# A selective scan's decay kept in PSUM: the exponential written over its input, three banks deep

## The reference, cut to what matters

```python
xn = layernorm over channels; each image gives 4 sequences (16 channels each) of 3136 tokens
xi, z = split(in_proj(xn));  u = silu(causal_conv4(xi) + conv_b)
dt, B, C = split(x_proj(u)); delta = softplus(dt_proj(dt) + dt_proj_b)
# per token, inner channel d (32) and state n (16):
dA = exp(delta * A);  h = h * dA + delta * u * B;  y = sum_n(h * C)
out = xn + out_proj((y + u * D) * silu(z))
```

## Time and profile before

| what | us |
|---|---|
| median of 3 runs | 11573.08 |
| lowest and highest | 11567.66, 11573.26 |
| span of the profiled execution, first to last instruction | 11567.8 |
| VectorE busy in it | 9091.6 |
| TensorE busy in it | 9063.4 |
| GpSimd busy in it | 7746.9 |
| ScalarE busy in it | 5494.1 |

### The profile page before, as it was taken

One profiled execution on the slowest core, in us unless ns is written; L12 is line 12 of the kernel. 1 busy time (PEld: TensorE's weight loads), 2 busy tenths in 40 slices (PEclk: granted clock), 3 DMA queues, 4 the chain that ended last, 5 costly groups with the idle time before them and its releaser, 6 DMA issues. The chain is left out here.

```text
span 11567.8 us, 144078 instructions
## 1 busy us (share of the span) xinstructions
PE 9063.4 (78%) x34187; PEld 4489.7 (39%) x34187; DVE 9091.6 (79%) x10036; ACT 5494.1 (47%) x9098; POOL 7746.9 (67%) x4490
## 2 busy tenths in 40 slices
PE   9967777777777777777777777777777799999997
PEld 9922222222222222222222222222222259996997
DVE  7769999999999999999999999999999912221222
ACT  0345555555555555555555555555555502320332
POOL 0059999998989999999989898999989800000000
PEclk9978888888888888888888888888888899999998
DMA  9611010101111111101010111111110110012002
GB/s 175 172 41 30 26 32 24 33 25 30 26 30 26 30 28 27 30 25 33 23 34 24 31 28 28 29 28 29 27 31 24 43 46 0 0 26 59 0 0 44
DMA packets 644710, 403.63 MB, mean 35 GB/s; under 512 B 399312, under 2 KB 631120, under 8 KB 643664
## 3 DMA queue, kind: packets, MB, share of 16 engines
q1 hardware_dynamic: 407888, 318.19, 11.0%
q10 hardware_dynamic: 236032, 77.08, 2.9%
HBM read 136.43 MB, written 103.80 MB: 21 GB/s over the span
## 5 line engine op out<-in xcount | busy, mean ns | idle before, releaser
L627 POOL TENSOR_TENSOR prod<-hs,bsp 128x448 f32<-128x448 f32 x3584 | 6395.7, 1817 | 333.9 <-PE ps L637 224.9
L615 DVE TENSOR_TENSOR_SCAN hs<-da,hs,dbu 128x448 f32<-128x448 f32 x3072 | 4423.0, 1440 | 0.0
L595 ACT ACTIVATE da<-ps,nega 128x448 f32<-128x448 f32 x3586 | 2201.2, 632 | 1741.2 <-PE ps L578 1607.3
L587 PE MATMUL ps<-stack,seld 96*128 96x448 bf16 x3586 | 1488.3, 415 | 1855.6 <-DVE dbu L605 1835.4
L605 DVE TENSOR_TENSOR dbu<-ps,bsp 128x448 f32<-128x448 f32 x3585 | 2148.5, 599 | 413.1 <-PE ps L587 398.1
L637 PE MATMUL ps<-prod,wc 128*32 128x448 f32 x7200 | 1763.8, 658 | 330.2 <-POOL prod L627 325.2
L587 PEld LDWEIGHTS ps<-stack,seld 96*128 96x128 bf16 x3586 | 357.1, 100 | 3753.0 <-DVE dbu L605 3284.4
L877 PE MATMUL ps<-pv,ws 128*128 128x224 f32 x8800 | 1692.3, 354 | 9.4 <-ACT pv L1030 7.1
L877 PEld LDWEIGHTS ps<-pv,ws 128*128 128x128 f32 x8800 | 1656.6, 188 | 45.7 <-issue 7.8
L578 PE MATMUL ps<-stack,seld 96*128 96x448 bf16 x3587 | 1482.0, 413 | 68.1 <-ACT da L595 67.8
L1211 DVE SCALAR_TENSOR_TENSOR pv<-ps,R 128x224 f32<-128x224 f32 x880 | 422.2, 480 | 1279.3 <-PE ps L877 1279.3
(11 more groups left out here) (120 smaller groups left out, 9271.4 us busy)
## 6 DMA issues: line engine op xcount, KB each, us to landing
stack<-parts SPq DMA_DIRECT2D x2700, 56.0 KB, 2.0
lnx<-in_x SPq DMA_DIRECT2D x118, 224.0 KB, 2.5
lny<-y_nchw SPq DMA_DIRECT2D x118, 224.0 KB, 2.7
x_column_pairs<-otile SPq DMA_DIRECT2D x225, 116.0 KB, 1.7
xpad<-x_column_pairs SPq DMA_DIRECT2D x32, 812.0 KB, 4.4
xpad<-in_x SPq DMA_DIRECT2D x64, 392.0 KB, 6.7
y_pairs<-yout ACTq DMA_DIRECT2D x32, 784.0 KB, 6.8
yin<-y_pairs SPq DMA_DIRECT2D x32, 784.0 KB, 4.4
```

Source lines behind the costliest of these rows:

```text
L587: pe.matmul(ps[:, DU_BANK + j % 2, 0:T], seld[0:96, b, :], stack[:, st.t % 2, 1, grp, :], start=True, stop=True).then_inc(S["du_spread"], 1)
L595: a.activation(da[:, j % 8, :], ps[:, D_BANK + j % 2, 0:T], ACT.Exp, scale=nega[:, j:j + 1])\
L615: v.tensor_tensor_scan(hs[:, j, :], da[:, j % 8, :], dbu[:, j % 8, :], 0.0 if first else hs[:, j, T - 1:T], ALU.mult, ALU.add)\
L627: g.tensor_tensor(prod[:, j % 8, :], hs[:, j, :], bsp[:, st.t % 2, 1, :], ALU.mult)\
```

## The change

The exponential is written in place, over its input in PSUM, and the scan reads it there. Three banks (0 to 2) take the part of two banks and of the eight SBUF buffers `da`, which go. As unit i of a round of 224 uses bank i % 3 and 224 is no multiple of 3, `d_bank_back` finds how many units back a bank was used last: three, and at the start of a round two (units 0, 1) or five (unit 2). `spread_delta` now waits for the scan of that unit and no longer for an exponential; `decay` waits for its matmul alone. To free a bank, `project_out` writes to bank 7, which the state sums (`Y_BANK`) now use too, and the first matmul of the sums also waits for the copies out of that bank. `project` moves from TensorE's step 8 to step 5, `sum0` from 7 to 8, and `evacuate` from ScalarE's step 12 to step 6.

```diff
-PE_AT = {0: ["bc0", "last3"], 3: ["bc1"], 5: ["lnc"], 7: ["sum0"], 8: ["project", "lnv"], 10: ["tap0", "tap2"],
+PE_AT = {0: ["bc0", "last3"], 3: ["bc1"], 5: ["project", "lnc"], 8: ["sum0", "lnv"], 10: ["tap0", "tap2"],
          12: ["tap1"], 13: ["tap3", "sum1", "z", "dt"], 14: ["sum2"]}
-ACT_AT = {1: ["bc0"], 2: ["relu"], 4: ["bc1"], 5: ["cast0"], 7: ["cast1"], 8: ["lnc"], 11: ["lnv"],
-          12: ["shift", "evacuate"], 14: ["silu", "u", "z", "exp"], 15: ["dt"]}
+ACT_AT = {1: ["bc0"], 2: ["relu"], 4: ["bc1"], 5: ["cast0"], 6: ["evacuate"], 7: ["cast1"], 8: ["lnc"], 11: ["lnv"],
+          12: ["shift"], 14: ["silu", "u", "z", "exp"], 15: ["dt"]}
...
-            da = sb(m, "da", [P, 8, T])
...
-        D_BANK, DU_BANK, TMP_BANK, Y_BANK, O_BANK = 0, 2, 4, 6, 7
+        D_BANK, DU_BANK, TMP_BANK, Y_BANK, O_BANK = 0, 3, 5, 7, 7
+        ROUND = ST * UN
+
+        def d_bank(st, j):
+
+            return D_BANK + (st.t * UN + j) % 3
+
+        def d_bank_back(st, j):
+
+            i = st.t * UN + j
+            back = [m for m in range(i - 5, i) if (m % ROUND) % 3 == i % 3]
+            return i - back[-1]
...
-            pe.wait_ge(S["exp_done"], st.tile * UN + j + 1)
-            pe.matmul(ps[:, D_BANK + j % 2, 0:T], seld[0:96, b, :], stack[:, st.t % 2, 0, grp, :],
+            pe.wait_ge(S["scan_done"], st.tile * UN + (j + 9 - d_bank_back(st, j)))
+            pe.matmul(ps[:, d_bank(st, j), 0:T], seld[0:96, b, :], stack[:, st.t % 2, 0, grp, :],
...
-            a.wait_ge(S["scan_done"], n + 1)
-            a.activation(da[:, j % 8, :], ps[:, D_BANK + j % 2, 0:T], ACT.Exp, scale=nega[:, j:j + 1])\
+            d = ps[:, d_bank(st, j), 0:T]
+            a.activation(d, d, ACT.Exp, scale=nega[:, j:j + 1])\
...
-            v.tensor_tensor_scan(hs[:, j, :], da[:, j % 8, :], dbu[:, j % 8, :],
+            v.tensor_tensor_scan(hs[:, j, :], ps[:, d_bank(st, j), 0:T], dbu[:, j % 8, :],
...
                 pe.wait_ge(S["y_gated"], tile + 2)
+                pe.wait_ge(S["out_evac"], tile * 2 + 3)
```

## The result

| | us |
|---|---|
| kernel before, median of 4 | 11573.17 |
| changed kernel, median of 4 | 11782.98 |
| ratio, with its 95% interval | 1.0184 (1.0169 to 1.0198) |
| span of the profiled execution | 11783.4 |

The forecast was 11280 us, faster. The kernel became 210 us slower; the time lies inside the range, the direction is wrong.

The account below looks back on a forecast made before the run. VectorE was taken as the bound, its scans taking turns with GpSimd's multiplies. Own work 29.9, full-clock waits 4.1 and low-clock waits 2.7 gave 36.7 us a tile against 37.96, hence 11280 us; range 10850 to 11920.

Parts of the forecast that it names:

- own work: VectorE's operations in one tile without its waits for TensorE, forecast at 29.9 us a tile.
- Part 1: Scan's first input moves to PSUM: scan and drive together fall from 1.88 to 1.57 us, 16 save 5.0 us a tile.
- turn: VectorE operations with two SBUF inputs and GpSimd's own exclude each other; scan and multiply about 0.95 us each.
- Part 2: TensorE's new wait for a scan delays drive: 4.1 us a tile at full clock, 2.7 us extra at lower clock.
- step 10: Two taps on TensorE, covered by VectorE's scale in half the tiles: 0.4 us of full-clock wait a tile.
- steps 13, 0, 5, 8, 10: Full-clock waits behind TensorE's tasks: 2.8, 0.6, 0, 0.1 and 0.4 us a tile, in that order.
- low-clock and round shares: Extra TensorE waits: 2.7 us a tile from 1.2 GHz, 0.2 from bank reuse where a 14-tile round ends.
- step 8: TensorE's sum0 and lnv, 2.4 us, partly covered by rest at 1.35: 0.1 us full-clock wait, 1.2 extra at low clock.
- the gap between project and sum0: Three steps now part these TensorE tasks; before, they adjoined and brought the clock up. Low clock adds 2.7 us a tile.
- Rival A: TensorE's queue becomes the bound, at steps 5 to 13: 40.0 us a tile, +460 us, about 12030 us; chance 0.26.
- B: TensorE's clock stays up, the low-clock extra goes: 34.0 us a tile, -890 us, about 10680 us; chance 0.14.
- C: The scan keeps taking turns with GpSimd despite PSUM: 41.3 us a tile, +740 us, 12310 us; chance 0.05.

Follow-up runs that it names:

- the first experiment: The changed kernel with ScalarE's two layer-norm operations (lnv) at step 10 instead of 11: 11473.06 us, ratio 0.9922 against the kernel before.

## Why the prediction was wrong, point by point

The forecast was 36.7 us a tile, measured were 38.9. The 2.2 us between them are 1.1 for a wait that the forecast did not have (the scale's), 1.3 more for TensorE (8.1 against 6.8), and 0.2 less of own work.

**Part 1 was right.** Unit 1.57 us as forecast: counted in the trace, scans follow each other by 1.56 to 1.57 us where nothing waits. At the scan no turn is left and no price of PSUM shows: the least scan from PSUM took 1071 ns, from SBUF 1073. The forecast's estimate from the Trainium skill ("VectorE: DVE Perf Modes", "The TRN2 errata"), 65 ns more for each scan from PSUM, is not borne out by these two rows. Own work came to 29.7 us against 29.9; the second `rest` took 1068 ns, less than I gave it; in the timeline above GpSimd stands still beside it, waiting for TensorE.

**Part 2's mechanism was right, its list was not complete.** This step failed: "Behind it in TensorE's queue stand the tasks of step j and then `spread_du`". Behind the delta matmul stands also the exponential, and behind that ScalarE's tasks. I followed ScalarE only to scan 18 and, at step 10, let VectorE's `scale` cover the taps, without asking what the scale itself waits for: that wait stands in the forecast at nothing, and took 1.1 us a tile. Undoing this one coupling gives 310 us and turns the sign: 11473 us is faster than before by 0.8%. It is the difference between the right and the wrong direction, though not all of the error.

**The waits for TensorE were sized too low**: 6.8 us a tile forecast; 8.1 measured, 7.4 with the scale's coupling undone. Counted by unit in that run and set against my terms (steps 13, 0, 5, 8, 10 are felt at units 0, 3, 8, 11, 13): 3.3 against 3.2 with the low-clock and round shares, 0.7 against 0.6, 0.6 against 0.7, 1.9 against 1.3, 0.7 against 0.8. The mis-sized term is step 8: sum0 and lnv hold the queue for 3.9 us in the timeline above (mean granted clock there 0.65), and the second `rest` that was to cover them lasts 1.07 us, spaced 0.99, and not 1.35.

**The clock** was granted at 0.77 from 1.3 to 8.5 ms (0.84 before). It lengthens TensorE's tasks: the skip's 1.70 us above was run at a granted 0.50. How much of the waits that makes, no run parts from the order. That the gap between project and sum0 was its cause was argued only. The moves alone lower it to 0.80 and the wait alone to 0.74, while putting project back beside sum0 left it at 0.80: so both the moves and the wait bear on it, and the gap is not shown to.

**Rival A** has the direction and only half of the reason. It wanted TensorE's queue to cost more than 8.1 us a tile. It cost just 8.1, and with 29.7 us of own work that alone is 37.8 us, no change. The 0.9 us above 37.96 come with the scale's 1.1, which A did not have, and its 40.0 us were not reached. B and C did not occur.

Open: what share of the 172 us that TensorE's waits lost in the first experiment is the clock's and what the order's, was not parted. A version in which ScalarE's softplus no longer delays the exponentials was not tried, nor the evenly spread tasks with the scan from SBUF.

## What to carry to other kernels

When a result is written in place over its input, the wait for the last reader moves one engine up the chain: here from ScalarE, which wrote the buffer, to TensorE, which feeds ScalarE. Walk down every queue that stands behind that wait, not the nearest alone, and look for a task whose consumer comes earlier in its own queue than the thing it now waits for. Then put the work that nobody waits for ahead of the waiting instruction: here three such edits gave 929 us once the scan was fast, and nothing while it was slow; spreading the tasks evenly gave another 375.

## What the runs showed of the hardware that I had not expected

- A VectorE operation with two SBUF inputs that alternates with GpSimd's can cost the other engine more than itself: with the scan's first input in PSUM the scan fell from 1440 to 1138 ns, and the multiply from 1817 to 1220 ns, 2114 us in all.
- The scan with one PSUM and one SBUF input and a pointer scalar to SBUF varied by 12 ns over 3072 operations beside a GpSimd that was busy 4282 us with multiplies. So the pointer scalar takes no turn that shows.
- ScalarE's exponential was a little shorter with its output in PSUM (607 ns) than in SBUF, where it took 632, each on average over 3586 operations.
